# One block of a graph network on one Trainium2 core: the eight expert weight sets laid out in groups of 32 rows and summed on TensorE in narrow column groups

## The reference, cut to what matters

```python
gh = relu(x @ gfc1_w.T + gfc1_b)                       # "gate"
g = (gh @ gfc2_w.T + gfc2_b).mean(over the 1250 rows)  # 8 numbers
W1m = W1 + sum over e of g[e] * tv_W1[e]               # 256 x 512
W2m = W2 + sum over e of g[e] * tv_W2[e]               # 512 x 256
b1m = b1 + g @ tv_b1;  b2m = b2 + g @ tv_b2
h = relu(x @ W1m.T + b1m)                              # "ffn1"
out = h @ W2m.T + b2m                                  # "ffn2"
res = x + out, then a layernorm of res
```

## Time and profile before

| what | value |
|---|---|
| median of 3 runs | 506.99 us (506.45 to 510.55) |
| the profiled execution's own time | 507.89 us |
| its span, first to last instruction | 506.1 us |
| mean granted TensorE clock over the span | 0.979 of full |

### The profile page before, as it was taken

The page is one execution under the profiler, slowest core; times in us unless marked ns, Lnnn a source line. Parts: engine busy times, 40 slices in busy tenths (PEclk is TensorE's granted clock), DMA queues, the critical chain, the costliest instruction groups (busy, mean ns, idle before and its releaser), DMA issues.

```text
span 506.1 us, 9887 instructions
## 1 busy us (share of the span) xinstructions
PE 465.9 (92%) x3564; PEld 361.1 (71%) x3564; DVE 325.5 (64%) x749; ACT 250.2 (49%) x524; POOL 166.6 (33%) x176
## 2 busy tenths in 40 slices
PE   2979999999999998998999998999999979989892
PEld 1868568886765676666999984678998758956651
DVE  4658798747999857754655357625333675439787
ACT  4688355147712345335434755425346377734454
POOL 1369343111095003033227970004232113304513
PEclk9999999999999899999999998999999979989998
DMA  8700102202020002021100001000000295000014
GB/s 246 208 1 29 56 0 85 85 1 83 1 85 0 2 3 84 0 82 48 41 0 1 0 13 50 1 0 1 0 3 4 83 413 253 1 0 2 1 53 150
DMA packets 5247, 27.44 MB, mean 54 GB/s; under 512 B 1037, under 2 KB 1162, under 8 KB 3545
## 3 DMA queue, kind: packets, MB, share of 16 engines
q1 hardware_dynamic: 5208, 26.92, 15.2%
HBM read 24.36 MB, written 2.56 MB: 53 GB/s over the span
## 4 chain that ended last, share of the span: by engine, by line
PE 76%; DVE 14%; ACT 5%; issue 3%; POOL 1%; DMA 1%; SPq 0%; ACTq 0%; DVEq 0%
PE ps L460 47%; PE ps L632 17%; PE ps L449 4%; PE ps L726 3%; PE ps L525 2%; PE ps L535 1%; DVE r L1666 1%; DVE late L1169 1%; DVE r L1168 1%; DVE r L1678 1%; PE ps L446 1%; POOL late L1719 1%; DVE r L1656 1%; DVE ohs L1159 1%; DVE offsets L1154 1%
## 5 line engine op out<-in xcount | busy, mean ns | idle before, releaser
L460 PE MATMUL ps<-r,wslot 128*128 128x250 f16 x840 | 97.6, 276 | 4.4 <-DVE r L1168 4.3
L460 PEld LDWEIGHTS ps<-r,wslot 128*128 128x128 f16 x840 | 82.7, 100 | 16.8 <-DVE r L1168 6.1
L632 PE MATMUL ps<-late,r 125*128 (+1 forms) x800 | 87.1, 269 | 1.4 <-DVE r L1388 1.4
L632 PEld LDWEIGHTS ps<-late,r 125*128 125x128 f16 x800 | 77.4, 97 | 11.4 <-issue 2.1
L1727 POOL TENSOR_TENSOR wslot<-stage,wslot 128x512 f16<-128x512 f32 x32 | 39.6, 1268 | 135.8 <-ACT wslot L778 135.8
L460 PE MATMUL ps<-wslot,r 128*125 128x512 f16 x300 | 70.5, 386 | 0.0
L460 PE MATMUL ps<-wslot,late 128*125 128x512 f16 x240 | 56.5, 389 | 3.2 <-DVE late L1460 2.7
L460 PEld LDWEIGHTS ps<-wslot,r 128*125 128x125 f16 (+1 forms) x300 | 40.9, 139 | 22.1 <-issue 1.4
L1755 POOL TENSOR_TENSOR late<-ohs,late 128x250 f16<-128x250 f32 x40 | 25.7, 652 | 90.5 <-ACT late L954 90.5
L460 PE MATMUL ps<-late,wslot 128*128 (+1 forms) x480 | 51.7, 269 | 0.0
L460 PEld LDWEIGHTS ps<-late,wslot 128*128 128x128 f16 x480 | 46.6, 97 | 5.3 <-issue 0.8
(11 more groups left out here) (183 smaller groups left out, 729.3 us busy)
## 6 DMA issues: line engine op xcount, KB each, us to landing
late<-in_tv SPq DMA_DIRECT2D x2, 4096.0 KB, 17.5
x<-in_x SPq DMA_DIRECT2D x5, 448.0 KB
out<-r SPq DMA_DIRECT2D x10, 224.0 KB
stage<-in_w_up SPq DMA_DIRECT2D x2, 1024.0 KB, 5.2
stage<-in_w_down SPq DMA_DIRECT2D x2, 1024.0 KB, 5.5
stage<-in_w_lin SPq DMA_DIRECT2D x1, 1024.0 KB, 6.2
stage<-in_w_k SPq DMA_DIRECT2D x1, 1024.0 KB, 4.9
stage<-in_w_q SPq DMA_DIRECT2D x1, 1024.0 KB, 4.7
```

Source lines behind the costliest of these rows:

```text
L460: last = nc.tensor.matmul(out, stat_(hs, b), mov(hm, b), start=start and n == 0, stop=stop and n == 3 * blocks - 1)
L632: last = nc.tensor.matmul(bank("t", m), u_nat[layer][:, p, h, m * 128:(m + 1) * 128], counts(h)[:, chunk], start=(start and h == 0 and p = ...
```

## The change

Each expert matrix has 128 rows. The change stores it in `tv` so that the 128 partitions hold four groups of 32: partitions 0 to 31 hold experts 0 and 4, partitions 32 to 63 experts 1 and 5, and so on. The 128 rows of one expert become four blocks of 32 rows side by side. The load is now 16 transfers of 512 KB, each into 32 partitions, in rows of 4 KB. With experts stacked over the partitions, one matmul sums four experts at once: `g_stack` (128 by 32) has g of the partition's own expert where the row within the group matches. Its result is 32 rows of the merged part, written to 32 partitions of the bank: four matmuls (j = 0 to 3) with 32 stationary columns fill a bank, and two sets of four experts make eight matmuls per part. PE so sums all eight experts. DVE makes `g_stack` (two small products with an accumulated sum, two of 128 by 32; two masks are made earlier), and ACT's `g_diag` goes. DVE's only work per part is to add the bank to the base weights.

Orders change too: on PE the bias b2 matmul moves from between the W1 parts to after ffn1 m = 0, ACT does `high_w1(1)` before the first `hidden`, and both `high_w2` after i = 4. On POOL the b2 instructions move to after i = 4. W1 part 1 uses bank 4 and W2 part 0 bank 5.

The diff, cut to its core:

```diff
@@ -74,8 +74,9 @@
...
 AT_ONCE = 5
-PE_EXPERTS = 4
-PE_SHARE = (4, 3, 4, 3)
+GROUP = 32
+GROUPS = 128 // GROUP
+SETS = E // GROUPS
 S_B, LOW_ROW = 64.0, 32
@@ -220,8 +221,14 @@
...
         tvrow = ohs[0:E, 2 * KB * CH:2 * KB * CH + 6 * D].bitcast(F32).rearrange("e (r c) -> e r c", r=3)
-        g_diag = ohs[:, 2 * KB * CH + 6 * D:2 * KB * CH + 6 * D + PE_EXPERTS * 256].bitcast(F32).rearrange(
-            "p (e n) -> p e n", e=PE_EXPERTS)
+        gate_at = 2 * KB * CH + 6 * D
+        def gate_tile(at, n):
+            return ohs[:, gate_at + at:gate_at + at + 2 * n].bitcast(F32)
+        g_stack = gate_tile(0, SETS * GROUP).rearrange("p (s i) -> p s i", s=SETS)
+        of_group, in_group = gate_tile(128, GROUP), gate_tile(192, GROUPS)
+        g_own, g_picked = gate_tile(208, SETS), gate_tile(224, E).rearrange("p (s e) -> p s e", s=SETS)
         b2_ones = ohs[:, OHS - 128:OHS]
@@ -414,8 +421,11 @@
...
             sp.wait_ge(full["t"], before("t", "gate"))
+            grouped = dram["tv"].rearrange("(j i) w e n -> i w j e n", j=GROUPS)
             for w in range(2):
-                sp.dma_start(tv[:, w], dram["tv"][:, w]).then_inc(got_tv, 16)
+                for e in range(E):
+                    own, at = slice(e % GROUPS * GROUP, (e % GROUPS + 1) * GROUP), e // GROUPS * GROUPS
+                    sp.dma_start(tv[own, w, at:at + GROUPS, :], grouped[:, w, :, e, :]).then_inc(got_tv, 16)
             for t in range(T):
@@ -719,33 +729,34 @@
...
 
-            def merge_on_pe(bank_, part, share):
-                for k in range(PE_EXPERTS - share, PE_EXPERTS):
-                    pe.wait_ge(diag_ready, k + 1)
-                    last = nc.tensor.matmul(bank_, g_diag[:, k, :], part(E - PE_EXPERTS + k), start=(k == PE_EXPERTS - share),
-                                            stop=(k == PE_EXPERTS - 1))
+            def merge_on_pe(bank_, part):
+                for set_ in range(SETS):
+                    pe.wait_ge(diag_ready, set_ + 1)
+                    for j in range(GROUPS):
+                        last = nc.tensor.matmul(bank_[j * GROUP:(j + 1) * GROUP], g_stack[:, set_, :], part(GROUPS * set_ + j),
+                                                start=(set_ == 0), stop=(set_ == SETS - 1))
                 last.then_inc(pe_merged, 1)
...
                 merge_on_pe(ps[:, bank_, :].rearrange("p (k f) -> p k f", k=KB),
-                            lambda e: tv[:, 0, e, :].rearrange("p (k f) -> p k f", k=KB)[:, :, m * 128:(m + 1) * 128], PE_SHARE[m])
+                            lambda e: tv[:, 0, e, :].rearrange("p (k f) -> p k f", k=KB)[:, :, m * 128:(m + 1) * 128])
 
             def merge_w2(bank_, h):
-                merge_on_pe(ps[:, bank_, :], lambda e: tv[:, 1, e, h * D:(h + 1) * D], PE_SHARE[FB + h])
-            pe.wait_ge(got_tv, 32)
+                merge_on_pe(ps[:, bank_, :], lambda e: tv[:, 1, e, h * D:(h + 1) * D])
+            pe.wait_ge(got_tv, 32 * E)
             wait_done(pe, "y", "gnn", T)
             merge_w1(6, 0)
-            pe.wait_ge(g_vec, 1)
-            nc.tensor.matmul(ps[0:P, 7, :], grow[:, :], tvrow[:, 2, :], start=True, stop=True).then_inc(b2_sum, 1)
-            merge_w1(5, 1)
+            merge_w1(4, 1)
             for m in range(FB):
...
                 if m == 0:
-                    merge_w2(4, 0)
+                    pe.wait_ge(g_vec, 1)
+                    nc.tensor.matmul(ps[0:P, 7, :], grow[:, :], tvrow[:, 2, :], start=True, stop=True).then_inc(b2_sum, 1)
+                    merge_w2(5, 0)
                     merge_w2(6, 1)
@@ -756,7 +767,7 @@
...
 
-            return sum(2 * (E - n) + 1 for n in PE_SHARE[:part + 1])
+            return part + 1
 
@@ -1074,10 +1085,6 @@
...
 
-            act.wait_ge(g_col, 1)
-            for k in range(PE_EXPERTS):
-                e = E - PE_EXPERTS + k
-                nc.scalar.activation(g_diag[:, k, :], ident[:, :], ACT.Copy, scale=gcol[:, e:e + 1]).then_inc(diag_ready, 1)
             def high_w1(part):
@@ -1091,12 +1098,12 @@
...
             act.wait_ge(b1_done, 1)
+            high_w1(1)
             for i in range(FB * J):
                 hidden(i)
-                if i == 1:
-                    high_w1(1)
-                if i in (J - 1, 2 * J - 2):
-                    high_w2(int(i > J))
+                if i == J - 1:
+                    high_w2(0)
+                    high_w2(1)
             def scale_unit(u):
@@ -1573,6 +1580,8 @@
...
 
+            then(nc.vector.tensor_reduce(of_group[:, :], ident[:, :].rearrange("p (e i) -> p i e", e=GROUPS), AX.X, ALU.add))
+            then(nc.vector.tensor_reduce(in_group[:, :], ident[:, :].rearrange("p (e i) -> p e i", e=GROUPS), AX.X, ALU.add))
             wait_done(dve, "t", "gate", 20)
@@ -1581,28 +1590,19 @@
...
             dve.wait_ge(g_col, 1)
+            for set_ in range(SETS):
+                last = nc.vector.scalar_tensor_tensor(g_picked[:, set_, :], gcol[:, GROUPS * set_:GROUPS * (set_ + 1)], 1.0,
+                                                      in_group[:, :], ALU.mult, ALU.mult, accum_out=g_own[:, set_:set_ + 1])
+            then(last)
+            for set_ in range(SETS):
+                nc.vector.tensor_scalar(g_stack[:, set_, :], of_group[:, :], g_own[:, set_:set_ + 1], None, ALU.mult
+                                        ).then_inc(diag_ready, 1)
             dve.wait_ge(got_wm, 16)
-            dve.wait_ge(got_tv, 32)
-            half_done = [0]
-            def merge(total, task, experts):
-                halves = [(total[:, k:k + n], lambda e, k=k, n=n: task(e)[:, k:k + n])
-                          for n in [total.shape[1] // 2] for k in (0, n)]
-                for e in range(experts):
-                    for h, (out, part) in enumerate(halves):
-                        if e:
-                            dve.wait_ge(merged, half_done[0] + 2 * e + h - 1)
-                        nc.vector.scalar_tensor_tensor(out, part(e), gcol[:, e:e + 1], out, ALU.mult, ALU.add).then_inc(merged, 1)
-                half_done[0] += 2 * experts
-                dve.wait_ge(merged, half_done[0])
             def add_pe_part(total, bank_, n):
...
                 nc.vector.tensor_tensor(total, bank_, total, ALU.add).then_inc(merged, 1)
-                half_done[0] += 1
-                dve.wait_ge(merged, half_done[0])
+                dve.wait_ge(merged, n)
 
@@ -1612,7 +1612,6 @@
...
 
-            merge(w1_part(wm32[:, 0, :], 0), lambda e: w1_part(tv[:, 0, e, :], 0), E - PE_SHARE[0])
             wait_full(dve, "x", "g", 1)
@@ -1624,27 +1623,20 @@
...
             nc.vector.tensor_scalar(b1m[:, :], b1m[:, :], S_X, None, ALU.mult).then_inc(b1_done, 1)
-            merge(w1_part(wm32[:, 0, :], 1), lambda e: w1_part(tv[:, 0, e, :], 1), E - PE_SHARE[1])
-            add_pe_part(w1_part(wm32[:, 0, :], 1), ps[:, 5, :].rearrange("p (k f) -> p k f", k=KB), 2)
+            add_pe_part(w1_part(wm32[:, 0, :], 1), ps[:, 4, :].rearrange("p (k f) -> p k f", k=KB), 2)
+            low_w1(1)
             dve.wait_ge(b2_sum, 1)
...
                                     ).then_inc(b2_added, 1)
-            low_w1(1)
 
...
                 return slice(h * D, (h + 1) * D)
-            def merge_w2(h):
-                merge(wm32[:, 1, half(h)].rearrange("p (k n) -> p k n", k=2),
-                      lambda e: tv[:, 1, e, half(h)].rearrange("p (k n) -> p k n", k=2), E - PE_SHARE[FB + h])
 
...
 
-            merge_w2(0)
-            add_pe_part(wm32[:, 1, half(0)], ps[:, 4, :], FB + 1)
-            merge_w2(1)
+            add_pe_part(wm32[:, 1, half(0)], ps[:, 5, :], FB + 1)
             low_w2(0)
@@ -1788,7 +1780,7 @@
...
 
-            for i in range(2):
+            for i in range(J):
                 low_hidden(i)
@@ -1800,7 +1792,7 @@
...
             pool.wait_ge(b2_ready, 2)
-            for i in range(2, FB * J):
+            for i in range(J, FB * J):
                 low_hidden(i)
...
             pool.wait_ge(xb_ready, T)
```

## The result

The median is 501.1 us (500.75 to 503.35, four runs) beside 506.8 us (506.45 to 510.55) for the kernel before: a ratio of 0.988 with the interval 0.985 to 0.991. The change makes the kernel 1.2% faster; 0.3% slower was forecast. The profiled execution took 501.0 us, of which 499.0 us is span, 7.1 less than before.

The account below looks back on a forecast made before the run. The prediction took PE, busy for 92% of the span, as the bound. Its terms +0.83 (W1), +2.16 (b2 and W2) and -1.34 (ffn2's wait) summed to +1.65, so 508.6 us, with a range of 500.5 to 516.

Parts of the forecast that it names:

- The sums: PE's expert sums: 32 narrow records for two parts, between 8 slots and 32, taken as 17.
- 17 slots: PE's sums for two parts: in program order two records share a slot, 16 and one to fill, 7.31 us.
- the lower bound: PE's sums for two parts: if the four column groups run at once, 32 records cost 8 slots.
- 10 slots for four: PE's sums: the skill page read as a gain of 3.17 for four tiles, making 32 records some 10 slots.
- W1, +0.83 forecast: From W1's sums to ffn1 with m = 0: 9.85 us in place of 9.02, so ffn1 begins 0.83 later.
- rival 1: PE's sums: all four column groups run at once, W1 limited by its weight chain; -5.35, so 501.6 us; chance 0.20.
- The start of the sums, +0.4 forecast: Making the gates' matrix on DVE: ready 0.96 after g, so PE starts the sums 0.4 later, at 450.96.
- b2 and W2, +2.16 forecast: b2 and W2's sums on PE: 0.86 and 7.31, 8.17 in place of 6.01, another 2.16 us.
- ffn2's wait, -1.34: PE's idle ahead of ffn2, put down to DVE's last low half: the 1.34 us are gone.
- The load, hidden: Load of 8.39 MB in 16 transfers of 32 partitions: 47.0 us available, hidden down to 179 GB/s.
- The sum: Whole kernel: +0.83 + 2.16 - 1.34 = +1.65, so 508.6 us, 0.3% slower.

Follow-up runs that it names:

- group_outer: Changed kernel with the two loops of the expert sums exchanged, all of one column group before the next: 501.77 us, ratio 0.986 to the kernel before.
- four_per_group: Changed kernel with W2's sixteen matmuls ordered by column group over both parts, eight records of one group in a row: 508.43 us, one run.
- wide_8: Changed kernel's orders with the old layout and load, all eight experts summed on PE with 128-wide diagonal matrices: 522.37 us, one run.
- load_128_rows: Changed kernel with the old load, two transfers of 4096 KB into all 128 partitions (merged weights wrong): 501.35 us, ratio 0.986 to the kernel before.
- dve_adds_out: Kernel before with DVE adding only one of its four or five experts in each part: 508.08 us, ratio 0.999 to the kernel before.
- w2_high_late: Changed kernel with ACT's second `high_w2` put back behind the ninth hidden chunk: 502.98 us, ratio 0.989 to the kernel before.

## Why the prediction was wrong, step by step

**The sums: the step that failed.** "If PE starts matmuls in program order, group 1 can then overlap only with the second record of group 0" was a condition that no row bore out, and I took its 17 slots, 7.3 us for W2, as the value. Measured are 8 slots (3.57 to 3.64 us), the lower bound that the prediction also names; `group_outer` and `four_per_group` show that the condition does not hold, and `wide_8` that the rest of the price was right: wide records take a slot each, as a lone narrow one does. The Trainium skill, TensorE: Matmul & The Clock Gate, says in its part on packing small matmuls that matmuls start and end in program order. The two runs of other orders speak against it for the starts on different column groups; the ends were not looked at. Its 2.38 times for three tiles, from which the prediction estimated 10 slots for four, falls short of what was measured here: 3.8 times for four, 8 slots.

**W1, +0.83 forecast.** Measured -4.83 in the first profile, -3.2 to -3.6 in the others by starts of the sums. At 8 slots PE's sums no longer set ffn1's start; the weight chain does (L1604, L1091, L1176 in the chain above), as rival 1 says. PE idles for 0.19 to 0.55 us ahead of ffn1 in six of the seven profiles that have this order and the load in time; in `load_128_rows`, with the clock low, it doesn't idle, so the two ends lie close together. What the prediction says of the clock, that the loss stays, is right for all profiles of the changed layout but the first.

**The start of the sums, +0.4 forecast.** From g's last instruction to the first sum there were 0.75 us and are now 0.88, counted from its start: +0.13. The forecast set the two products one after the other; they start at 450.22 and 450.31. `g_stack` then follows at 450.51.

**b2 and W2, +2.16 forecast.** Measured -1.29: b2 costs 1.05 (0.86 forecast, by slots; its row already says 1.05), W2 3.57 in place of 6.01. The rest, 0.1, lies in how the starts are read.

**ffn2's wait, -1.34.** The size is right (-1.50, the wait and some spacing), the cause wrong; it came out because the change also moves ACT's instruction. The low half that ends the wait did come from DVE, but `dve_adds_out` takes the additions away and the wait stays, and `w2_high_late` brings it back by ACT's order alone. The prediction named the last releaser and did not follow the chain one link further, to L1090 behind the ninth hidden chunk, though DVE's own 1.51 us of idle stood in the same trace.

**The load, hidden.** Right, and by the margin: over by 445 where 450.9 was needed. 8.39 MB at some 210 GB/s are 40 us, above the 179 that suffice. The Trainium skill, SBUF — State Buffer, under Door 1, has the rate follow the ports that the written partitions reach, with 189 GB/s for 32 and 104 for 16 at 1 MiB, and limits of about 218 and 109. The traces agree in kind, with 392 to 419, 207 to 220 and 129 GB/s for 128, 32 and 16 rows; for 16 rows the measured rate lies above the page's limit, and the measurement decides.

**The sum.** Rival 1, given 0.20, was what happened: 501.6 forecast, 501.1 measured. That it is so near is partly luck. Its terms for W1, W2 with b2, and the wait were -2.3, -1.71 and -1.34, where the repeated profiles have -3.1 to -3.5 (with the later start), -1.3 and -1.5. (Its end of part 0, 454.7, should also read 454.4: 450.96 and four slots of 0.86.) With the failed step put right, by the repeated profiles: +0.1, -3.2 to -3.6, -1.3, -1.5 are -5.9 to -6.3, and the three ratios of the change (0.988, 0.988, 0.989) are 5.5 to 6.2 us. So about three quarters of the gain are the sums, and some 1.5 us are ACT's order: my first theory, that the sums are all of it, gave them too much. The range held the median; the chances did not, since 0.55 lay on no change.

## What to carry to other kernels

Where many small sums of the form diagonal times matrix stand on PE, stacking them over the partitions and giving each column group of 32 its own part made them 3.8 times cheaper here, where the program order changed group after two or four records; after eight it was lost in large part, and nothing between was run. A releaser's name is where a wait ends, not where it comes from: follow it back until an engine that was busy all the time. And where a cost is bounded from both sides by a condition that no row shows, the gap between the bounds belongs in the chances.

## What the runs showed of the hardware

An fp32 record of 512 columns starts 0.43 us after the one before at the full clock, whether it has 128 or 32 stationary columns, if both use the same columns. Records on four different column groups run side by side: 32 of them took 3.64 us, against 14.00 us wide. The reach across groups is short: four records of one group in a row cost nothing (3.68 us), eight did (8.86 us). The DMA share is full at 410, 208 and 129 GB/s alike, so the rate must be read beside it. The clock granted in 451 to 456 was 0.66 to 0.76 in all profiles of the changed kernel and its variants with the load in time, but for the first, which had 1.00 with the same idle time ahead of the sums (0.61 us, and 0.60 in the next); why is open. In 405 to 415 it was 0.83, 0.61 and 0.53 in the three profiles of the changed kernel, and the first sum behind it started at 450.9, 451.7 and 449.6: not later for the lower clock.
